# Four relations of a graph layer as seven half-size products each, the sort in two relations, padding rows out of bounds

## The reference, cut to what matters

```python
def _rgcn(x, edge_index, edge_type, weight, root, bias):     # x 1250x1024, weight 8x1024x1024
    src, dst = (edge_index[0], edge_index[1])                # 21250 edges
    msgs = x[src]
    out = x @ root + bias
    for r in range(weight.shape[0]):
        mask = (edge_type == r).astype(x.dtype)
        sums = jax.ops.segment_sum(msgs * mask[:, None], dst, num_segments=n)
        cnt = jax.ops.segment_sum(mask, dst, num_segments=n)
        mean = sums / jnp.maximum(cnt, 1.0)[:, None]
        out = out + mean @ weight[r]
    return out
u = _rgcn(layernorm(x), ...)
z = jnp.concatenate([u, x], axis=1) @ w_gate + b_gate
h = jnp.tanh(u) * z + x * (1.0 - z)
# x = x + h; then x = x + top-2 of 8 SwiGLU experts of layernorm(x)
```

## Time and profile before

| what | value |
|---|---|
| median of 3 runs | 1887.54 us (1886.41 to 1888.28) |
| profiled execution, own time | 1879.97 us |
| its span, first to last instruction | 1877.9 us |
| TensorE busy | 1760.9 us, 94% |
| VectorE, ScalarE, GpSimd busy | 962.8, 595.3, 639.2 us |
| mean granted TensorE clock | 0.973 |

### The profile page before, as it was taken

How to read it: one execution, slowest core, us unless ns; L and a number is a source line. 1 busy time by engine, 2 the same in 40 slices (tenths; PEclk the granted TensorE clock), 3 DMA queues, 4 the chain that set the end, 5 groups by cost and what they waited for, 6 DMA issues and landing times. The chain is left out here.

```text
span 1877.9 us, 22607 instructions
## 1 busy us (share of the span) xinstructions
PE 1760.9 (94%) x8113; PEld 1448.1 (77%) x8113; DVE 962.8 (51%) x1166; ACT 595.3 (32%) x850; POOL 639.2 (34%) x535
## 2 busy tenths in 40 slices
PE   7999999999999999999999999999889967999993
PEld 6888888888888888888777777777668855787882
DVE  8545555655410110010079999998889976434300
ACT  2211111111111111111156656655532212455451
POOL 1000000000166666610055555555355523545531
PEclk9999999999999999999999999999989977999997
DMA  5222222222532222222188888888754445777645
GB/s 199 90 96 90 79 74 73 84 73 79 171 106 92 93 84 90 84 84 89 62 279 265 302 269 294 265 269 281 239 213 168 157 155 197 191 218 187 160 82 152
DMA packets 122552, 292.80 MB, mean 156 GB/s; under 512 B 16084, under 2 KB 32516, under 8 KB 122384
## 3 DMA queue, kind: packets, MB, share of 16 engines
q1 hardware_dynamic: 80592, 161.17, 24.3%
q0 software_dynamic: 41872, 130.44, 23.7%
HBM read 213.92 MB, written 82.76 MB: 158 GB/s over the span
## 5 line engine op out<-in xcount | busy, mean ns | idle before, releaser
L585 PE MATMUL banks<-whi,xhi 128*128 128x512 f32 x1280 | 502.0, 392 | 0.6 <-DVE xlo L473 0.6
L586 PE MATMUL banks<-wlo,xhi 128*128 128x512 f32 x1280 | 498.9, 390 | 0.0
L587 PE MATMUL banks<-whi,xlo 128*128 128x512 f32 x1280 | 498.9, 390 | 0.0
L732 POOL DMA_INDIRECT gathered<-Y,edge_row x184 | 220.8, 1200 | 317.5 <-PE banks L846 180.7
L309 ACT ACTIVATE y_out<-banks 128x512 f32<-128x512 f32 x160 | 95.5, 598 | 717.8 <-PE banks L587 717.8
L358 DVE TENSOR_TENSOR wlo<-w_stage,whi 128x1024 fp32r<-128x1024 f32 x66 | 80.7, 1224 | 459.6 <-ACT whi L301 458.9
L585 PEld LDWEIGHTS banks<-whi,xhi 128*128 128x128 f32 x1280 | 240.8, 188 | 50.6 <-DVE xlo L473 1.2
L587 PEld LDWEIGHTS banks<-whi,xlo 128*128 128x128 f32 x1280 | 240.7, 188 | 50.3
L586 PEld LDWEIGHTS banks<-wlo,xhi 128*128 128x128 f32 x1280 | 240.8, 188 | 49.0
L751 ACT ACTIVATE ghi<-gathered,edge_w 128x1024 fp32r<-128x1024 f32 x184 | 211.3, 1152 | 170.1 <-DMA gathered<-Y,edge_row 164.6
L789 DVE SCALAR_TENSOR_TENSOR glo<-gathered,edge_w,ghi 128x1024 fp32r<-128x1024 f32 x184 | 232.2, 1281 | 42.8 <-ACT ghi L751 42.3
(11 more groups left out here) (254 smaller groups left out, 2385.5 us busy)
## 6 DMA issues: line engine op xcount, KB each, us to landing
Y<-y_out SPq DMA_DIRECT2D x160, 256.0 KB, 2.0
w_stage<-in_L_gnn_weight SPq DMA_DIRECT2D x62, 512.0 KB, 3.6
raw<-in_L_ffn_w SPq DMA_DIRECT2D x24, 1024.0 KB, 9.4
YX<-y_out SPq DMA_DIRECT2D x40, 256.0 KB, 5.1
w_stage<-in_L_gnn_w_gate SPq DMA_DIRECT2D x12, 512.0 KB, 7.0
X<-x SPq DMA_DIRECT2D x11, 512.0 KB, 3.0
acc<-in_L_gnn_bias POOLq DMA_DIRECT2D x10, 512.0 KB, 10.3
u<-YX SPq DMA_DIRECT2D x10, 512.0 KB, 5.0
```

The lines of the kernel that those rows point to most:

```text
L585: pe.matmul(psum[slot][:], xhi[:, k, at], whi[h][:, k], start=(k == 0), stop=False)
L586: pe.matmul(psum[slot][:], xhi[:, k, at], wlo[h][:, k], start=False, stop=False)
L587: ins = pe.matmul(psum[slot][:], xlo[:, k, at], whi[h][:, k], start=False, stop=(k == KC - 1))
L732: nc.gpsimd.indirect_dma_start(out=gath[:, t % GR], out_offset=None, in_=Y, in_offset=bass.IndirectOffsetOnAxis(ap=edge_row[:, t:t + 1], a ...
```

## The change

**Relations 0 to 3** stay full-size. **Relations 4 to 7** are each computed by the scheme of Strassen in Winograd's form: x is cut into quarters of 640 rows by 512, the weights into quarters of 512 by 512, and seven products of sums of quarters stand in for eight products of quarters. A product is 5 tiles x 4 chunks x 3 = 60 matmuls of 128x512 (12 for each tile), a relation 7 x 60 = 420. Products are numbered n = 0 to 27, n % 7 being the place in the scheme. The sums of weights are made by GpSimd (`t_load`, `t_make`, `t_store`: 32 steps, each with four additions of 128x256 in SBUF, two loads and two stores of 256 KB) and go to device memory (`TW`). The sums of x are made by VectorE in additions of 128x2560, ten before the last tile of relation 3 and eight after it. A quarter of x is saved in device memory after relation 0 and brought back during product 25.

The right factors come in chunks of 128x512 through three buffers (`raw_chunk`), are split by ScalarE and VectorE (`chunk_hi`, `chunk_lo`) into a ring of two products, one product ahead. Results are combined by VectorE (`sum_tile`) out of the banks, and stored by SyncE (`store_quarter`). **The root weights** for the third block are loaded and split in the last product (`root_part`, `root_low`).

**The sort** runs in relations 1 and 2, 12 groups in each, spread evenly over the product steps. **`acc`** is set after product 25 instead of before the edge weights. **Padding rows** get a row number past the end of Y, and the gather skips what is past its bound (R * NP - 1). The loops over relations are unrolled.

```diff
-        CPQ = 7
-        SORT_R = ECOLS // (8 * CPQ)
-        assert SORT_R * 8 * CPQ == ECOLS
+        CPQ, SORT_R = 7, 2
+        SG1 = ECOLS // (SORT_R * CPQ)
...
+        TS, TQ = 3, HALF // 2
+        t_set = z2b.put("t_set", [P, TS, 2, 2, TQ], F32)
...
+        LEFT = ((quarter(xhi, 0, 0), quarter(xlo, 0, 0)), (quarter(xhi, 0, 1), quarter(xlo, 0, 1)),
+                (s2hi, s2lo), (quarter(xhi, 1, 0), quarter(xlo, 1, 0)), (s4hi, s4lo), (s3hi, s3lo),
+                (quarter(xhi, 1, 1), quarter(xlo, 1, 1)))
...
+        def right(n, k):
+
+            r, p = R0 + n // 7, n % 7
+            w = TW[(r - R0) * D:(r - R0 + 1) * D, :] if p in (2, 3, 5, 6) else weight[r]
+            low, wide = p in (1, 4, 5, 6), p in (3, 4, 5)
+            return w[low * HALF + k * P:low * HALF + (k + 1) * P, wide * HALF:(wide + 1) * HALF]
...
+                            if last and h == 0 and j == NT - 2:
+                                sp.wait_ge(w_lo, R0 * 8)
+                                for c in range(raw_n):
+                                    load_raw(c)
+                            if last and h == 1 and j < 8:
+                                load_raw(raw_n + j)
...
+                def load_raw(c):
+                    n, k = c // KH, c % KH
+                    if c >= raw_n:
+                        sp.wait_ge(q_lo, c - raw_n + 1)
...
+                    if n == SN - 1:
+                        sp.wait_ge(hy_out[0], 16 * 3 * (R - R0))
+                        sp.wait_ge(hy_out[1], 16 * 2 * (R - R0))
+                        sp.wait_ge(q_lo, KH * SN)
+                        load(R0, 0, 0, True)
+                        load(R0, 0, 1, True)
+                    for i in range(TR):
+                        if i < len(ahead):
+                            load_raw(ahead[i])
+                        store_quarter(n, i)
+                        if n == SN - 1 and i in (1, 2):
...
+                def chunk_hi(c):
+                    n, k = c // KH, c % KH
...
+                    if n >= 2 and k == 0:
+                        act.wait_ge(tile_done, TR * (n - 1))
+                    nc.scalar.activation(ring_hi[n % 2][:, k], raw[:, c % raw_n], ACT.Copy).then_inc(q_hi, 1)
...
+                def root_part(q):
+                    place, arrived, count = staged(R0, 0, q)
+                    act.wait_ge(arrived, count)
+                    act.wait_ge(tile_done, TR * (SN - 1))
+                    nc.scalar.activation(whi3[:, 2 * q:2 * q + 2, :], place, ACT.Copy).then_inc(w_hi, 1)
...
+                SPLIT_PARTS = (0, 1, 3, 4)
...
-                        for q in range(4):
...
-                                columns(r, 4 * h + q, first and h * 4 + q == 0)
...
+                                columns(r, h * SG1 // 2 + part, r == 1 and h == 0 and part == 0)
+                            if part in SPLIT_PARTS and not (start and h == 0):
+                                split_lo(*((r, 1) if h == 0 else (r + 1, 0)), SPLIT_PARTS.index(part))
...
-                step(v.scalar_tensor_tensor(edge_row[:], tfl[:, 0], float(NP), placed[:, 0], ALU.mult, ALU.add))
+                step(v.scalar_tensor_tensor(tfl[:, 3], tfl[:, 0], float(NP), placed[:, 0], ALU.mult, ALU.add))
+                step(v.tensor_scalar(tfl[:, 2], edge_dst[:], 0.5, float(NO_ROW), ALU.is_lt, ALU.mult))
+                step(v.tensor_tensor(edge_row[:], tfl[:, 3], tfl[:, 2], ALU.add))
...
+                for i in range(TS):
+                    dve.wait_ge(t_moved[i], t_stored[i])
+                dve.wait_ge(inv_out, 16)
+                step(both(s4sum, a21h, a21l, ALU.add))
+                step(both(s4sum, s4sum, a22h, ALU.add))
+                step(both(s4sum, s4sum, a22l, ALU.add))
+                chunk_lo(0)
...
+                chunk_lo(3)
...
+                step(both(s3sum, a11h, a21h, ALU.subtract))
+                step(both(s3sum, s3sum, a21l, ALU.subtract))
+                both(s3sum, s3sum, a11l, ALU.add).then_inc(s_raw, 1)
+                dve.wait_ge(x21_moved, 32)
+                step(both(s1sum, a21h, a21l, ALU.add))
+                step(both(s1sum, s1sum, a22h, ALU.add))
+                both(s1sum, s1sum, a22l, ALU.add).then_inc(s_raw, 1)
...
+                def sum_tile(n, i):
...
+                    if p == 6:
+                        ins = v.tensor_tensor(half_u[i][:], bank[:], half_u[i][:], ALU.add)
+                    ins.then_inc(summed, 1)
...
+                def root_low(q):
+                    dve.wait_ge(w_hi, R0 * 8 + q + 1)
+                    v.tensor_tensor(wlo3[:, 2 * q:2 * q + 2, :], staged(R0, 0, q)[0],
+                                    whi3[:, 2 * q:2 * q + 2, :].bitcast(F32), ALU.subtract).then_inc(w_lo, 1)
...
+                for n in range(SN):
+                    for i in range(TR):
+                        if 1 <= n < SN - 1 and i < KH:
+                            chunk_lo(KH * (n + 1) + i)
+                        if n == SN - 1 and i < 4:
+                            root_low(i)
+                        if n % 7 >= 2:
+                            sum_tile(n, i)
...
+                def t_load(m):
+                    if m >= TS:
+                        pool.wait_ge(t_moved[m % TS], 64 * (m // TS))
+                    s, k, part = m // 8, m // 2 % KH, m % 2
...
+                        rows_of = weight[R0 + s][a * HALF + k * P:a * HALF + (k + 1) * P, :]
+                        pool.dma_start(t_set[:, m % TS, a], rows_of.rearrange("p (b n) -> p b n", b=2)
+                                       [:, :, part * TQ:(part + 1) * TQ]).then_inc(t_moved[m % TS], 16)
+
+                def t_make(m):
+                    pool.wait_ge(t_moved[m % TS], 64 * (m // TS) + 32)
+                    b11, b12, b21, b22 = (t_set[:, m % TS, a, b] for a in range(2) for b in range(2))
+                    nc.gpsimd.tensor_tensor(b22, b22, b12, ALU.subtract).then_inc(t_made, 1)
+                    nc.gpsimd.tensor_tensor(b12, b12, b11, ALU.subtract).then_inc(t_made, 1)
+                    pool.wait_ge(t_made, 4 * m + 1)
+                    nc.gpsimd.tensor_tensor(b11, b22, b11, ALU.add).then_inc(t_made, 1)
+                    pool.wait_ge(t_made, 4 * m + 3)
+                    nc.gpsimd.tensor_tensor(b21, b21, b11, ALU.subtract).then_inc(t_made, 1)
+
+                def t_store(m):
+                    s, k, part = m // 8, m // 2 % KH, m % 2
+                    pool.wait_ge(t_made, 4 * m + 4)
+                    for a in range(2):
+                        at = s * D + a * HALF + k * P
+                        pool.dma_start(TW[at:at + P, :].rearrange("p (b n) -> p b n", b=2)
+                                       [:, :, part * TQ:(part + 1) * TQ], t_set[:, m % TS, a]).then_inc(t_moved[m % TS], 16)
+
+                pool.wait_ge(hot_ready, 1)
+                t_load(0)
+                t_load(1)
+                for m in range(T_STEPS):
+                    t_make(m)
+                    if m + 2 < T_STEPS:
+                        t_load(m + 2)
+                    t_store(m)
...
-                    pool.dma_start(acc[:, j * D:(j + 1) * D], bias.partition_broadcast(P)).then_inc(acc_set, 16)
                 for t in range(ET):
...
                 pool.wait_ge(acc_set, 16 * NT)
...
             @block.tensor
             def _(pe):
-                def product(r, h, j, first=False):
...
+                        c = (h * NT + j) * KC + k
+                        part = c * SG1 // (2 * NT * KC)
+                        if sorts and (c + 1) * SG1 // (2 * NT * KC) > part:
+                            columns(r, part, r == 1 and part == 0, r == SORT_R and part == SG1 - 1)
...
+                for n in range(SN):
+                    p = n % 7
...
+                    if LEFT_READY[p]:
+                        pe.wait_ge(s_ready, LEFT_READY[p])
+                    for i in range(TR):
+                        bank_free(n, i)
+                        bank, at = psum[PRODUCT_BANKS[p][i]], slice(i * P, (i + 1) * P)
+                        for k in range(KH):
...
+                                pe.wait_ge(q_lo, KH * n + k + 1)
...
+                                      stop=False, skip_group_check=True)
+                            pe.matmul(bank[:], hi[:, k, at], ring_lo[n % 2][:, k], start=False, stop=False,
+                                      skip_group_check=True)
+                            ins = pe.matmul(bank[:], low[:, k, at], ring_hi[n % 2][:, k], start=False,
+                                            stop=(k == KH - 1), skip_group_check=True)
+                        ins.then_inc(tile_done, 1)
...
-                        in_offset=bass.IndirectOffsetOnAxis(ap=edge_row[:, t:t + 1], axis=0)).then_inc(g_in[t % GR], 16)
+                        out=gath[t % GR][:], out_offset=None, in_=Y,
+                        in_offset=bass.IndirectOffsetOnAxis(ap=edge_row[:, t:t + 1], axis=0),
+                        bounds_check=R * NP - 1, oob_is_err=False).then_inc(g_in[t % GR], 16)
```

323 lines of the change are left out of this document (258 added, 65 removed).

## The result

The changed kernel takes 1900.68 us (median; 1888.26 to 1914.57), the kernel before, run beside it, 1890.12 us. The ratio is 1.0065, with a 95% interval of 1.0045 to 1.0086: slower by some 11 us where 23 fewer were forecast. Some executions of the kernel before run for a stretch at half clock and take some per cent longer; they are left out of every ratio here, and no ratio is given where too few others stand beside a run.

A forecast was written before the change was run, and what follows sets the result against it. TensorE's matmul count was taken to bound the second block, the gather chain to idle TensorE in the third. Terms -54.4 + 21 + 11.5 + 1 (clock) - 2 = -22.9 us took the median from 1887.54 to 1864.6 us, range 1843 to 1890.

The forecast's parts named there:

- The matmuls: Relations 4 to 7: 28 products of 60 matmuls instead of 4 x 480, price per matmul kept; -54.4 us.
- rival C: Before product 0: sums of weights come late, at 13 us a step TensorE waits 56 us; 1908.6 us, chance 0.10.
- The additions: Sort in relations 1 and 2: GpSimd's sums of weights delay VectorE's one-hot tiles, TensorE waits; +21 us, bounds 0 and 65.
- The room: VectorE's slack in a sort group's period: 0.71 us with a low part of weights, 1.94 us without.
- Rival B: Sort: each addition costs VectorE its whole 0.74 us, +44 us in all; 1887.6 us, no change, chance 0.14.
- The end: Between the last product and the third block: late root weights lengthen the rest; +11.5 us, from 9 to 16.
- the chain: End of second block: third and fourth root-weight loads each wait behind a tile's sum and store, 7.0 us each.
- The third block: Gathers of the third block: skipped padding rows save little; -2 us, from -10 to 0, up to +17 if gathers lengthen.
- Rival E: Third block: the bound makes gathers slower, +17 us on the forecast; 1881.6 us, chance 0.06.

## Why the prediction was wrong, step by step

**The matmuls** (-54.4) were right: -54.4, with every bank, chunk and sum on time. Product 0 began without a wait, so the sums of x were hidden and rival C fell: the steps of `TW` ended near 393 us and not 411, `inv` came at 427.

**The additions** (+21, found +34.7) had the right mechanism and place and the wrong size, at one term: "I count 1.2 of them into the time in which VectorE waits for TensorE anyway, and 4 into its work, 2.0 us". The period held 6.0 additions and not 5.2, since a step took 8.1 us and not 8.9, and fewer of them were free: 14 of the 124 between 136 and 390 us lie wholly in VectorE's idle time, 11% and not 23%, and VectorE is idle for 1.3 of 12.05 us. They added 3.15 us. The room was underrated as well, 1.71 us against 0.71 or 1.94 (on average 1.12), which gave part of it back: 24 x (3.15 - 1.71) against 24 x (2.0 - 1.12). The price of one, 0.41 to 0.52 us from the earlier trace rows, was near: 0.53 with the idle ones counted in. Nor did the sum hold anything for the clock inside the sort; half clock behind the waits is 5.1 of the 34.7 us.

In single places it is the whole addition. VectorE's instruction of 896 elements, 1.08 us in the kernel without additions, beside GpSimd's additions:

```profile
208.18 3.83 DVE L538 TENSOR_TENSOR oh_klo<-iota,key_lo 128x896 bf16<-128x896 f32 x1
...
208.69 0.99 POOL L831 TENSOR_TENSOR t_set<-t_set 128x256 f32<-128x256 f32 x1
209.39 0.98 POOL L832 TENSOR_TENSOR t_set<-t_set 128x256 f32<-128x256 f32 x1
210.09 0.96 POOL L834 TENSOR_TENSOR t_set<-t_set 128x256 f32<-128x256 f32 x1
211.13 1.47 POOL L836 TENSOR_TENSOR t_set<-t_set 128x256 f32<-128x256 f32 x1
```

Three additions follow one another every 0.70 us, as fast as alone, 2.1 us in all, and a fourth begins 0.9 us before VectorE's instruction ends; that instruction is 3.83 - 1.08 = 2.75 us longer than alone. The Trainium skill, page SBUF — State Buffer, section Who interferes with whom, says that two SBUF inputs on VectorE and a reading GpSimd instruction contend for one exclusive lock, which whoever issues first keeps for its whole instruction. The length of this hold-up agrees; who issued first, the recorded starts don't show, since VectorE's lies 0.5 us ahead. The mean of 0.53 us for an addition of 0.73, part of them in idle time, is nearer to that rule than the prediction allowed. Rival B, which took that rule, had +44 us: its price for a group, 3.0 us, was close to the 3.15 found, and for this execution it was too high because the room was 1.71 us. Two of the other four executions came to +44.1 and +46.6.

**The end** (+11.5, found +20.1): the chain was right, its links were not. The second load landed 11.4 us after its issue (904.8 to 916.1) and not 6.5, although the prediction had the 10.3 us of an `acc` transfer in a full queue before it; it also left 2.5 us nearer to the last product's end; and the two links were 7.9 and 7.3 us, not 7.0. These are 4.9 + 2.5 + 1.2 = 8.6 us. I took the landing time between the alone one and the full one, while the prediction itself said that stores, chunks, `acc` and root weights run there together.

**The third block** (-2, found +12.0): the failed step is that the bound stood in the sum at nothing; its price was only an upper bound, "up to +17 if the comparison makes each gather 0.1 us or more longer". The gather did get longer (1200 to 1262 ns), and that was harmless; the cost, 9.4 us, is 0.5 us of later start from a register move that the rows of before could not show. Skipping the rows gave 4 to 6 us in this block, so the -2 itself was too small. Rival E had the size and the sign, with a chance of 0.06, and the wrong link. The trace of before had no gather with a bound, so the honest range for a new form of an instruction on this chain was the full one, with its middle above zero: the gain could be 10 us at most and the loss 17.

**What stays open.** Without a bound the third block of the change takes 421.7, 422.0 and 423.0 us in three kernels, 5.4 to 6.7 more than before. The traces say where it goes and not why. Half clock is 1.7 to 3.6 us of it (3.1, 4.8 and 5.0 us against 1.4), in the last because of two stretches of 3.4 us at 1270 and 1301 us, each beside a wait of 2.2 to 2.5 us. The waits for `glo` are 2.2 to 4.1 us more (23.4, 21.6 and 21.5 against 19.3). The change also places the gather buffers elsewhere and adds tensors behind `Y`; neither was tried. The scatter of relations 1 to 3 is one of waits and half clock; why they fall differently in like code was not found.

Three terms failed on the same side, so the time left the range. Two stayed within the upper bounds in the text (34.7 of 65 us, 12.0 of 17), the third did not (20.1 against 16); the range, up to 1890, was that of cases in which only one of them goes wrong.

## What to carry to other kernels

When GpSimd work is put beside a VectorE pipeline with two inputs in SBUF, count up to its whole length as VectorE's (0.53 of 0.73 us here on the mean), against the slack of one period, and widen the period where the work runs: here the same additions cost 35 to 47 us at 9.07 us of matmuls between groups and 6 to 13 at 10.9. Order the loads of the next block ahead of stores that wait for the last results, and don't let a bulk transfer share those microseconds. And pass the bound of an indirect transfer in a register that is written once: a constant was moved again in front of each of the 184 gathers, and where a ring of buffers has no slack, each move puts the ring off.

## What the runs showed of the hardware

A bound on an indirect gather, given as a constant, brings a 29 ns move whose price is 0.5 us of the gather's start; the gather itself is recorded at 1173 to 1200 ns on the mean in the five kernels without a bound and at 1206 to 1273 in the nine with one, too near to tell comparison from skipping; and skipping brings its data 0.1 to 0.35 us earlier (ScalarE starts 5.73 to 5.89 us after the gather's start, and 6.00 to 6.08 without). GpSimd's recorded lengths beside VectorE are not its pace: additions recorded at 0.96 to 0.99 us start 0.70 us apart. The Trainium skill, page Perfetto Trace Analysis, section GPSIMD Engine Instruction, advises to time GpSimd by the spacing of its starts; this stretch agrees. A 512 KB load lands in 3.6 us in the kernel before, in 3.9 and 4.5 in the rest between the blocks, in 5.0 at a DMA share of 0.85 to 0.91 and in 11 at 1.02. With waits of TensorE of 2.4 to 3.2 us in the sort the granted clock stood at half for 3.4 us in three places, and after the rest of 23 us it stayed at half until 4 us into the next block.
